# One fold of a fused attention kernel goes a step later: the first projection of the second pass runs ahead of it, and a small set-up moves with it

## What is computed

```python
def _L0_attn_a_ref(inputs_q, Wq, bq, Wk, bk, Wv, bv, Wo, bo):
    q, k, v = ...                      # inputs_q @ W + b, split into 16 heads of 16
    q = _feature_map(q)                # elu(x) + 1
    k = _feature_map(k)
    kv = jnp.einsum('bkhd,bkhm->bhdm', k, v)
    out = jnp.einsum('bqhd,bhdm->bqhm', q, kv)
    normalizer = jnp.maximum(jnp.einsum('bqhd,bkhd->bqh', q, k), EPS)
    return (out / normalizer[..., None]).reshape(B, S, D) @ Wo + bo

x = x + _L0_attn_a_ref(_layernorm(x), ...)
x = x + _L0_ffn_ref(_layernorm(x), ...)
x = x + _L0_attn_b_ref(_layernorm(x), ...)   # changes the first 16 tokens of a batch, adds a row to the others
x = x + _L0_ffn_ref(_layernorm(x), ...)
```

## Time and profile before

| | |
|---|---|
| median of 3 runs | 424.65 us (422.33 to 427.17) |
| profiled execution, its own time | 426.88 us |
| its span, first to last instruction | 425.1 us |
| PE busy | 404.6 us, 95% of the span |
| DVE, ACT, POOL busy | 71%, 52%, 67% |
| mean granted TensorE clock | 0.976 |

### The profile page before, as it was taken

The page is one execution under the profiler, slowest core; times in us unless marked ns, Lnnn a source line. Parts: engine busy times, 40 slices in busy tenths (PEclk is TensorE's granted clock), DMA queues, the critical chain, the costliest instruction groups (busy, mean ns, idle before and its releaser), DMA issues.

```text
span 425.1 us, 7528 instructions
## 1 busy us (share of the span) xinstructions
PE 404.6 (95%) x2586; PEld 343.9 (81%) x2586; DVE 301.7 (71%) x658; ACT 219.0 (52%) x386; POOL 286.7 (67%) x322
## 2 busy tenths in 40 slices
PE   8799999999999999969999999999999999999893
PEld 4688999998999899859888888678787878876662
DVE  6688889778876966563376779588648658776665
ACT  3577877776877674413545444234424433343431
POOL 3488867785878464453678778799557858857632
PEclk9989999999999999967999999999999999999998
DMA  7811111121100000233113333302320230231013
GB/s 248 270 52 50 51 52 49 51 54 47 51 0 2 2 0 2 79 91 115 56 26 85 107 103 105 103 22 84 104 80 31 100 106 18 87 103 54 5 47 109
DMA packets 31643, 29.80 MB, mean 70 GB/s; under 512 B 7766, under 2 KB 27484, under 8 KB 31580
## 3 DMA queue, kind: packets, MB, share of 16 engines
q1 hardware_dynamic: 31020, 28.50, 21.8%
q10 hardware_dynamic: 560, 0.52, 0.4%
HBM read 19.98 MB, written 8.98 MB: 68 GB/s over the span
## 4 chain that ended last, share of the span: by engine, by line
PE 79%; DVE 10%; issue 3%; ACT 3%; POOL 2%; DMA 1%; DVEq 0%; SPq 0%; POOLq 0%; ACTq 0%
PE PB L1573 10%; PE PT L1608 5%; PE PT L1470 5%; PE PA L1638 4%; PE PA L1639 3%; PE PA L1644 3%; PE PG L1426 3%; PE PG L1421 3%; PE PG L1422 3%; PE PA L1585 3%; PE PT L1648 2%; PE PT L1335 2%; PE PA L1380 2%; PE PA L1381 2%; PE PA L1382 2%
## 5 line engine op out<-in xcount | busy, mean ns | idle before, releaser
L534 POOL TENSOR_TENSOR o_lo<-q_all,o_hi 128x512 fp32r<-128x512 f32 x32 | 40.2, 1279 | 37.2 <-ACT o_hi L813 37.2
L1573 PE MATMUL PB<-ws,scratch 128*128 128x256 f32 x240 | 58.6, 387 | 1.2 <-DVE x_all L1163 1.2
L517 POOL TENSOR_TENSOR xn_pair<-scratch,xn_pair 128x512 fp32r<-128x512 f32 x32 | 41.3, 1290 | 23.2 <-ACT xn_pair L656 23.2
L1573 PEld LDWEIGHTS PB<-ws,scratch 128*128 128x128 f32 x240 | 43.8, 190 | 10.4 <-issue 5.4
L526 POOL TENSOR_TENSOR q_all<-q_all,scratch 128x512 f32<-128x512 f32 x32 | 40.5, 1284 | 9.9 <-DMA scratch<-inv_scratch 9.9
L1100 DVE BATCH_NORM_STATS2 ln_bn<-x_all 128x6 f32<-128x256 f32 x128 | 44.9, 413 | 0.9
L505 POOL TENSOR_TENSOR x_all<-x_all,wvo 128x1024 f32<-128x1024 f32 x16 | 44.4, 2774 | 0.0
L505 POOL TENSOR_TENSOR x_all<-x_all,ob_rows 128x1024 f32<-128x1024 f32 x16 | 37.7, 2354 | 0.0
L813 ACT ACTIVATE o_hi<-q_all 128x512 fp32r<-128x512 f32 x32 | 18.4, 623 | 37.3 <-PE PA L1644 35.8
L1154 DVE TENSOR_TENSOR x_all<-PA,x_all 128x1024 f32<-128x1024 f32 x16 | 19.6, 1223 | 24.5 <-PE PA L1644 24.5
L927 DVE TENSOR_TENSOR o_lo<-scratch,o_hi 128x512 fp32r<-128x512 f32 x32 | 31.8, 993 | 4.0 <-ACT o_hi L674 2.6
(11 more groups left out here) (280 smaller groups left out, 1172.6 us busy)
## 6 DMA issues: line engine op xcount, KB each, us to landing
scratch<-inv_scratch SPq DMA_DIRECT2D x32, 256.0 KB
x_all<-n_L_attn_a_inputs_q_dram SPq DMA_DIRECT2D x15, 512.0 KB, 3.6
out_dram<-x_all SPq DMA_DIRECT2D x15, 512.0 KB, 5.5
inv_scratch<-inv_turned SPq DMA_DIRECT2D x32, 16.0 KB
out_dram<-x_all SPq DMA_DIRECT2D x2, 256.0 KB, 2.3
x_all<-n_L_attn_a_inputs_q_dram ACTq DMA_DIRECT2D x2, 128.0 KB, 2.7
x_all<-n_L_attn_a_inputs_q_dram SPq DMA_DIRECT2D x2, 128.0 KB, 2.9
setup<-in_L_attn_a_Wq_dram ACTq DMA_DIRECT2D x1, 256.0 KB, 4.8
```

Source lines behind the costliest of these rows:

```text
L517: nc.gpsimd.tensor_tensor(halves[:, :, 1, :], pair(xn[n % 2], h), halves[:, :, 0, :].bitcast(F32), ALU.subtract).then_inc(x_lo, 1)
L534: nc.gpsimd.tensor_tensor(o_lo[:, c, :], q[:, c, :], o_hi[:, c, :].bitcast(F32), ALU.subtract).then_inc(o_lo_done, 1)
L1573: last = mm(four(dst)[:, t, :], h[:, t * P:(t + 1) * P], ws2[:, :], start=True, stop=True)
```

## The change

The fold of batch 3 from `kv_product` on goes from step 0 into step 1: `kv_product(3)` to the head of PE's step 1, `m_product(3)` behind L1617 there, and DVE's and ACT's parts with them, so that the projection of group 0 follows `fold_ffn_product`. Its buffers (the reloaded Wo, the copy of G) go from the scratch area to `folded_b`. The special tokens' set-up goes later: the DVE masks from slot (0, 1) to (1, 3), the block matrices from (0, 2) to (2, 1), the bias rows from (0, 3) to (2, 3), the weight products from (1, 1) and (1, 3) to (3, 1) and (3, 3). On SP, `inverse_rows(1)` goes ahead of the twelve short loads, and the four raw weights go into step 0 behind `inverse_rows(2)`.

```diff
 (SP, step)
                 if i + 2 < NG:
                     inverse_rows(i + 2)
+                if i == 0:
+                    for dst, w in zip(raw4, (qw, kw, vw, ow)):
+                        sp.dma_start(dst, rows(w)).then_inc(c_wts, 16)
 (SP, ahead of the steps)
             inverse_rows(0)
-            sp.wait_ge(t1_mm, NG)
-            sp.wait_ge(x_lo, 2 * NG)
+            sp.wait_ge(kq_mm, 2 * NG)
             sp.dma_start(wo_late, rows(Wo)).then_inc(wo_reloaded, 16)
-            sp.wait_ge(kq_mm, 2 * NG)
+            inverse_rows(1)
             for dst, w in zip(l_rows, (lqw, lkw, lvw)):
...
-            inverse_rows(1)
-            for dst, w in zip(raw4, (qw, kw, vw, ow)):
-                sp.dma_start(dst, rows(w)).then_inc(c_wts, 16)
 (ACT, chain: (0, 2) to (2, 1), (0, 3) to (2, 3), (1, 2) to (3, 1), (1, 3) to (3, 3); step:)
-                if i == 0:
+                if i == 1:
                     m_high(B - 1)
 (DVE, step)
-                if i == 0:
+                if i == 1:
                     batch_kv(B - 1)
                 if runs(v) and i != NG:
                     scaled_sum(i, v, nv)
                 chain(i, 1)
-                if i == 0:
-                    m_low(B - 1)
                 if runs(r):
...
                     nc.vector.tensor_tensor(h2s, h2, PT[:, 1, :], ALU.mult).then_inc(f1_scaled, 1)
+                if i == 1:
+                    m_low(B - 1)
 (DVE, chain: the masks from (0, 1) to (1, 3))
 (PE, step)
+                if i == 1:
+                    kv_product(B - 1)
                 if runs(r):
                     pe.wait_ge(w_added, r + 1)
...
                 if i == 0:
                     fold_ffn_product()
-                    kv_product(B - 1)
...
                 chain(i, 2)
-                if i == 0:
+                if i == 1:
                     m_product(B - 1)
 (PE, chain: (0, 2) to (2, 1), (0, 3) to (2, 3), (1, 1) to (3, 1), (1, 3) to (3, 3))
```

More of the change, by code:

```diff
@@ L161, in hybrid_kernel @@
         wo_early = late_q[:, 2 * D:4 * D].rearrange("p (c n) -> p c n", c=C)
-        late_x = x2t.rearrange("p c n -> p (c n)")
-        wo_late = late_x[:, 2 * D:4 * D].rearrange("p (c n) -> p c n", c=C)
         m_hi_last, m_lo_last = sb("m_hi_last", [P, C, D], F32R), sb("m_lo_last", [P, C, D], F32R)
@@ L168, in hybrid_kernel @@
         m_lo = [m_lo_early[:, b, :, :] for b in range(B - 1)] + [m_lo_last[:, :, :]]
-        g_flat = [late_q[:, 0:2 * D]] * (B - 1) + [late_x[:, 0:2 * D]]
-        g_sb = [g.rearrange("p (c n) -> p c n", c=C) for g in g_flat]
-        kvt = [g[:, 0:C * P].rearrange("p (c n) -> p c n", c=C) for g in g_flat]
         part = parts(sb("ffn_weights", [P, 2048])[:, :])
@@ L188, in hybrid_kernel @@
         folded_all = sb("folded_b", [P, 4 * C * D])[:, :]
+        wo_late = folded_all[:, 2 * D:4 * D].rearrange("p (c n) -> p c n", c=C)
+        g_flat = [late_q[:, 0:2 * D]] * (B - 1) + [folded_all[:, 0:2 * D]]
+        g_sb = [g.rearrange("p (c n) -> p c n", c=C) for g in g_flat]
+        kvt = [g[:, 0:C * P].rearrange("p (c n) -> p c n", c=C) for g in g_flat]
         token_of = sb("token_of", [P, B * P])
@@ L748, in chain @@
             def chain(i, slot):
-                if (i, slot) == (0, 2):
+                if (i, slot) == (2, 1):
                     act.wait_ge(c_bd, 1)
                     nc.scalar.activation(l_bd_all, PG[:, 0, 0:3 * P], ACT.Copy).then_inc(c_taken, 1)
-                elif (i, slot) == (0, 3):
+                elif (i, slot) == (2, 3):
                     act.wait_ge(c_brow, 1)
@@ L756, in chain @@
                     nc.scalar.activation(bias_k, PG[0:SP, 0, 3 * P:4 * P], ACT.Copy).then_inc(c_taken, 1)
-                elif (i, slot) == (1, 2):
+                elif (i, slot) == (3, 1):
                     act.wait_ge(c_fold, 1)
@@ L762, in chain @@
                                                  scale=col[:, c:c + 1]).then_inc(c_fold_sb, 1)
-                elif (i, slot) == (1, 3):
+                elif (i, slot) == (3, 3):
                     act.wait_ge(c_fold, 2)
@@ L1216, in chain @@
                 at = (i, slot)
-                if at == (0, 1):
+                if at == (1, 3):
                     dve.wait_ge(c_vecs, 16 * 12)
@@ L1670, in chain @@
                 at = (i, slot)
-                if at == (0, 2):
+                if at == (2, 1):
                     pe.wait_ge(c_blk, 4)
@@ L1675, in chain @@
                     last.then_inc(c_bd, 1)
-                elif at == (0, 3):
+                elif at == (2, 3):
                     pe.wait_ge(c_taken, 1)
@@ L1683, in chain @@
                     mm(PG[0:SP, 0, 3 * P:4 * P], l_col[:, 1:2].to_broadcast([P, SP]), center, start=True, stop=True).then_inc(c_brow, 1)
-                elif at == (1, 1):
+                elif at == (3, 1):
                     pe.wait_ge(c_wts, 16 * 4)
@@ L1691, in chain @@
                     last.then_inc(c_fold, 1)
-                elif at == (1, 3):
+                elif at == (3, 3):
                     pe.wait_ge(c_fold_sb, 2 * C)
```

## The result

The changed kernel takes 431.75 us (median of 4 runs, 431.33 to 432.06) against 423.49 us before (421.97 to 427.17): ratio 1.018, 95% interval 1.011 to 1.025. It is slower by 8.3 us; 430.2 us and a slower kernel were forecast. The profiled execution took 431.74 us, with a span of 430.0 us.

The account below looks back on a forecast made before the run. PE bounds the kernel, gapless in steps 1 to 4; -2.8 (earlier L1617) + 5.7 (moved work) + 2.6 (low clock) = +5.5 us on the median 424.65 gives 430.2 us, with an 8-in-10 range of 425.5 to 433.0.

Parts of the forecast that it names:

- What bounds the kernel: PE, busy 95% of the span; steps 1 to 4 have no gap in which moved work could hide.
- rival 4: A second wait: masks make step 2's rsq late, or block matrices wait for them; up to 2 us, 432 us, chance 0.08.
- Step 0: Projection of group 0 follows fold_ffn_product from 187.37 to 191.4 us; 1.4 us wait on w1c stays, 2.4 on masks goes.
- the 5 to 8 named as a sign: Sign of being right: a PE wait of 5 to 8 us ahead of L1617, released by DVE's L1110.
- The rows of group 2: Short loads on SP keep their load at 194.87, so rsq comes at 204.2 and PE waits some 7 us at L1617.
- The sum: Counted at L1617 of step 1: -2.8 + 5.7 + 2.6 = +5.5 us, put on the median.
- -2.8 us for the transposes of step 1: L1617 of step 1 starts at 204.2 in place of 207.04.
- The clock's 2.6 us: Loss from PE at half speed for 5.2 us behind the wait at L1617; bounds nothing and 5.0.
- The +5.7 us: Work not yet done at L1617: m_product 0.86, block matrices 0.83, bias rows 2.11, L1690 1.89.
- Rival 1: Nothing new is late: PE runs from 197.1 without pause at full clock; -4.2 us, 420.4 us, chance 0.10.
- Rival 2: Raw weights do not hold up group 2's rows: POOL's idle 1.51 us goes, rsq at 202.7; 428.7 us, chance 0.16.
- Rival 3: Clock stays up through the wait or returns within a microsecond: the 2.6 us fall away, 427.6 us, chance 0.06.

Follow-up runs that it names:

- experiment 10: The changed kernel itself, unaltered, run again beside one with PE's wait filled with matmuls: 431.90 us (6 runs), ratio 1.019 to the kernel before.
- experiment 7: Changed kernel with variances first on POOL, masks and token copy in other slots, w1c ahead of copy_g, raw weights behind inverse_rows(3): 422.18 us, ratio 0.995.
- experiment 11: The kernel before, unaltered, run for a second profile: 425.46 us.
- experiment 3: Changed kernel with the four raw weights issued in step 1 behind inverse_rows(3) instead of step 0 behind inverse_rows(2): 431.00 us, ratio 1.015.

## Why the prediction came out as it did

**What bounds the kernel.** Right. The later steps take moved work in full: the first layer's second product of step 1 starts at 209.74 in the changed kernel and at 212.34 before (212.51 in the chain), 2.6 us early, and the transposes of step 4 are 4.84 us late, so what lies between costs 7.4 us more. Counted were 6.2; 0.8 of the rest is a wait that was not in the sum (rival 4 below), and about 0.4 is not accounted for.

**Step 0.** Right in order, though PE was earlier than forecast. The projection of group 0 follows the fold of the feed-forward weights, from 185.15 to 188.07 us where 187.37 to 191.4 was forecast; the clock in this profile stayed up there, where half speed for a part of it was assumed. PE stands at its wait at 194.15 in place of 197, which makes the wait 9.0 us, outside the 5 to 8 named as a sign. As the text said, nothing of it reaches the end: in experiment 10 PE came at 196.9 and went on at the same time.

**The rows of group 2.** Right, instruction by instruction: the load at 193.75 (194.87 forecast), its halves used 3.90 and 6.73 us later (3.83 and 6.63), PE free at 203.18 (204.2). The offset of 1.05 us is the first pass, whose last transposed normaliser is ready that much earlier than in the earlier trace rows. Experiments 1, 2 and 4 show each link: without the short loads in between, with twice as many, and with the order on POOL exchanged.

**The sum.** The mechanism holds; the size came out too small, 5.5 us forecast against 8.3 between the medians. The term most at fault is the first one, -2.8 us for the transposes of step 1. It was read from a single execution that had PE there at 207.04 (206.88 in the timeline, which shows the same matmuls), while the shift was put on the median. In the other two profiles the timeline has them at 205.03 and 204.44, and the changed kernel's 203.18 is then 1.9 and 1.3 us early. The changed kernel stands on a floor, the time of `rsq`, that did not move with PE's clock (203.18 and 203.12 in its two profiles); the kernel before does not. The clock's 2.6 us were 1.6 in the profile and 1.9 in that of experiment 10. The +5.7 us held to the 0.4 above, with the 0.8 on top. With the profile of 424.39 us the same sum gives -1.3 + 5.7 + 1.6 + 0.8 = 6.8, against 7.4 measured.

Against the profile that it was worked out from, the change costs 4.9 us, and that 5.5 lies so near is partly luck. `rsq` came 1.05 us earlier than forecast and the clock cost 1.0 us less, while the 0.8 and the 0.4 us were not counted. The last 0.9 us from 7.4 to the medians' 8.3 lie in runs of the kernel before that no profile shows, and stay open. The 8.3 itself rests on 4 runs of the kernel before; its medians in the later experiments were 424.11 (19 runs), 424.34 (23) and 423.51 (11), against which 431.75 is 7.4 to 8.2 us more.

**The rivals.** Rival 1 (nothing new is late) falls; experiment 7 shows that it took five changes of order to get there, and 422.2 us in place of its 420.4. Rival 2 (the raw weights do not hold up the rows) falls for this load: POOL idles 1.57 us with them behind and 0.30 without. It is not so in every execution; the last section has one with them behind in which POOL idles 0.24 us. Rival 3 (the clock stays up) falls: it fell 5.3 us into the wait. Rival 4 (a second wait) is half right: step 2's `rsq` comes just in time, but the correction of that step waits 0.8 us on DVE, which has the copy for the tokens ahead of it.

**What the text did not see.** That moving the set-up is enough to open the wait. Experiment 6, the set-up alone, is 5.9 us slower at the median, most of the change's 8.3. The prediction priced the moved pieces where they arrive and did not ask what they had been covering where they stood. How much of the rest is the fold's is not shown, since the fold was not moved alone.

## What to carry to other kernels

Work on the bound engine that seems to be in the way may be the cover of a wait behind it: before moving it, find what the engine would wait for next and when that is ready. Follow every queue past which something moves, also one that is nearly idle: the issue time of small transfers counts, in order, against what stands behind them. And take a baseline from more than one profile before a gain or a loss is counted against it to a microsecond.

## What the runs showed of the hardware

The granted clock of a stretch does not tell how busy PE is in it, and it is not the same in each run of the same program. The kernel before ran at 0.50 from about 183.1 to 196.8 us in one profile, from 183.2 to 193.5 in another, and in that of experiment 11 from 184.4 to 187.8 and from 191.2 to 194.6. In the last one it came back to 1.00 for a stretch in which PE was busy for 0.55 of 3 us, and fell again in the next one, in which PE worked without a pause:

```profile
184.00:188.00 4.00, 3.56 (x16) 3.48 (x16) 1.23 (x4) 0.34 (x2) 0.00 (x0) 0.57 0.23 72
188.00:191.00 3.00, 0.55 (x5) 0.47 (x5) 2.36 (x6) 0.00 (x0) 1.97 (x2) 1.00 0.81 271
191.00:195.00 4.00, 4.00 (x20) 3.63 (x19) 0.69 (x1) 1.09 (x2) 0.63 (x1) 0.57 0.42 135
```

A load on SP's queue can be slowed by loads issued after it on the same queue. In the changed kernel the second half of the rows of group 2, 256 KB, was used 6.73 us after the issue of the pair with 1 MB behind it; in experiment 3 it was 5.09 us (194.25 to 199.34) without. This varies: over all profiles, where POOL stood waiting for the second half of group 1 or 2, it was used 5.3 to 6.7 us after the issue with the raw weights directly behind (ten loads), and 5.1 to 5.9 us without (eight loads). The shortest of the ten is that of group 1 in experiment 11, issued at 185.03:

```profile
190.36 1.27 POOL L526 TENSOR_TENSOR q_all<-q_all,scratch 128x512 f32<-128x512 f32 x1 [0.24 <-DMA scratch<-inv_scratch]
```
